# Attention's four key heads: a loop of one written pass and three repeated passes becomes four written passes on TensorE, ScalarE and VectorE

## The reference

```python
q = rope(x @ Wq + bq)   # 16 heads of 128, G = 4 query groups of HKV = 4 heads
k = rope(x @ Wk + bk)   # 4 key heads
v = x @ Wv + bv
scores = einsum('bgjtd,bjsd->bgjts', q, k) * scale      # j: the key head
wei = softmax(where(causal, scores, -inf))
out = einsum('bgjts,bjsd->bgjtd', wei, v)
x = layernorm(x + out @ Wo + bo)
x = layernorm(x + experts(x))     # top 8 of 64 experts per token
```

## Time and profile before

| what | us |
|---|---|
| median of 3 runs | 2161.45 |
| lowest and highest of them | 2160.99, 2162.3 |
| the profiled execution's own time | 2163.78 |
| span of the profiled execution, first to last instruction | 2162.0 |
| PE busy | 2042.1 (94%) |
| PEld busy | 1808.2 (84%) |
| DVE busy | 1679.5 (78%) |
| ACT busy | 1369.5 (63%) |
| POOL busy | 851.0 (39%) |
| mean granted TensorE clock | 0.978 |

### The profile page before, as it was taken

The page is one execution under the profiler, slowest core; times in us unless marked ns, Lnnn a source line. Parts: engine busy times, 40 slices in busy tenths (PEclk is TensorE's granted clock), DMA queues, the critical chain, the costliest instruction groups (busy, mean ns, idle before and its releaser), DMA issues. The chain is left out here.

```text
span 2162.0 us, 41335 instructions
## 1 busy us (share of the span) xinstructions
PE 2042.1 (94%) x13409; PEld 1808.2 (84%) x13409; DVE 1679.5 (78%) x3483; ACT 1369.5 (63%) x2747; POOL 851.0 (39%) x813
## 2 busy tenths in 40 slices
PE   8999989999999999999999999899959999999990
PEld 6888878998888988889888999788748999999990
DVE  5899987877678776787767877578877888888884
ACT  3677776766667666676656766332326877777773
POOL 1000013332233332333223333044455777787773
PEclk9999999999999999999999999999979999999995
DMA  7558553110531105301062000667637999999997
GB/s 241 189 209 287 217 210 111 61 64 21 158 115 41 59 21 174 111 30 59 22 225 99 29 21 21 241 242 287 235 112 218 298 299 297 296 292 293 296 250 257
DMA packets 140266, 362.62 MB, mean 168 GB/s; under 512 B 16304, under 2 KB 33328, under 8 KB 135472
## 3 DMA queue, kind: packets, MB, share of 16 engines
q1 hardware_dynamic: 111408, 292.09, 38.5%
q0 software_dynamic: 28672, 68.17, 13.2%
HBM read 224.27 MB, written 135.94 MB: 167 GB/s over the span
## 5 line engine op out<-in xcount | busy, mean ns | idle before, releaser
L654 PE MATMUL p_S<-p_kT,p_q 128*128 128x512 f32 (+3 forms) x1920 | 474.0, 377 | 14.0 <-ACT p_prob L732 12.0
L654 PEld LDWEIGHTS p_S<-p_kT,p_q 128*128 128x128 f32 x1920 | 324.2, 190 | 62.9 <-ACT p_prob L732 17.6
L843 POOL TENSOR_SCALAR p_prob<-p_prob,p_inv 128x128 f32<-128x128 f32 (+7 forms) x256 | 192.7, 753 | 452.3 <-DVE p_inv L792 452.3
L843 POOL TENSOR_SCALAR p_prob<-p_prob,p_inv,p_part 128x1024 f32<-128x1024 f32 x128 | 153.7, 1201 | 494.3 <-DVE p_inv L797 494.3
L666 PE MATMUL p_TP<-p_ident,p_prob 128*128 128x128 f32 x2176 | 303.6, 274 | 1.8 <-DVE p_pT1l L803 1.8
L781 DVE TENSOR_REDUCE p_nmax<-p_S 128x1 f32<-128x1024 f32 (+7 forms) x256 | 252.0, 984 | 22.8 <-PE p_S L654 21.8
L666 PEld LDWEIGHTS p_TP<-p_ident,p_prob 128*128 128x128 f32 x2176 | 245.5, 141 | 26.0 <-DVE p_pT1l L803 5.6
L741 ACT CAST p_pT0h<-p_TP 128x512 fp32r<-128x512 f32 (+3 forms) x320 | 155.3, 527 | 147.7 <-PE p_TP L666 146.6
L741 ACT CAST p_pT1h<-p_TP 128x512 fp32r<-128x512 f32 (+3 forms) x320 | 154.9, 526 | 145.7 <-PE p_TP L666 145.5
L1656 POOL DMA_INDIRECT sum_scratch<-p_y,p_tokT x128 | 212.9, 1663 | 55.7 <-issue 37.5
L689 PE MATMUL p_O<-p_pT1h,p_v 128*128 128x256 f32 x1088 | 225.9, 292 | 3.2 <-DVE p_pT0l L803 3.1
(11 more groups left out here) (228 smaller groups left out, 4555.8 us busy)
## 6 DMA issues: line engine op xcount, KB each, us to landing
p_w_raw<-in_gu SPq DMA_DIRECT2D x64, 768.0 KB
qk_scratch<-p_qout SPq DMA_DIRECT2D x80, 512.0 KB, 2.8
p_q<-qk_scratch SPq DMA_DIRECT2D x16, 2048.0 KB, 8.9
o_scratch<-p_oT SPq DMA_DIRECT2D x128, 256.0 KB, 2.1
p_ot<-o_scratch SPq DMA_DIRECT2D x32, 1024.0 KB, 7.4
p_w_raw<-in_gu SPq DMA_DIRECT2D x64, 256.0 KB
v_scratch<-p_vout SPq DMA_DIRECT2D x16, 512.0 KB, 3.2
p_t_raw<-in_dn SPq DMA_DIRECT2D x32, 256.0 KB
```

Of the source, the lines that this page charges most:

```text
L654: mm = nc.tensor.matmul(out, x, y, start=(n == 0), stop=(n == 2))
L843: nc.gpsimd.tensor_scalar(prob[k][:, cols], prob[k][:, cols], inv[:, k:k + 1], scale, ALU.mult, ALU.mult).then_inc(normed, 1)
```

## The change

`steps` no longer calls `loop`. The four heads are written out by Python for the three engines that call it, with j a number in all of them. GpSimd's loop and SyncE's loop stay as they are.

```diff
         def steps(eng, step, tail):
-            def body(j, first):
+            for j in range(HKV):
                 for i in range(U):
-                    step(j, i, first)
-            loop(eng, HKV, body)
+                    step(j, i, j == 0)
             for i in range(U, U + tail + 1):
                 step(HKV - 1, i, False)
```

## The result

Over 20 runs each the changed kernel has a median of 2158.07 us (2155.85 to 2162.29) and the kernel before 2161.82 us (2158.25 to 2163.98). The ratio is 0.9981, with a 95% interval of 0.9975 to 0.9988: the change gains 0.12 to 0.25%, or 2.6 to 5.4 us. That is clear over 20 runs each, but two single runs could not tell it, since the ranges overlap. The forecast was 2158.2 and a gain of 3.25 us; the medians differ by 3.75.

The account below looks back on a forecast made before the run. PE was taken as the bound, busy 2042.1 of 2162.0 us. From a median of 2161.45, -4.64 for branches and +1.39 for constants make -3.25, giving 2158.2 us; range 2154.8 to 2160.6.

Parts of the forecast that it names:

- The branches: Passages from head 1 to 2 and 2 to 3: without taken branches they lose 2.34 and 2.30 us, 4.64 in all.
- the second hole: Passage from head 1 to 2: PE idles 0.86 us for the key copy behind VectorE's branch; 0.98 us at the next.
- The constants: Heads 1 to 3: constants instead of registers in the waits cost 0.46 us per head, 1.39 us in all.
- Rival A: Heads 1 to 3: constants cost nothing, head 0's slower steps come from its place; 2156.8 us, chance 0.22.
- the hole at step 9: Head 3, step 9: PE waited 2.01 us, with a store late behind SyncE's 3 MB load; forecast to stay near 2.0.
- The fetch of the longer stream: Heads 1 to 3 as straight code: instruction fetching costed at nothing, covered by queued matmuls; otherwise up to 1.61 us per packet.
- Rival D: Heads 1 to 3: straight code starves PE, slower by over 0.2%; 2170.8 us at 0.3 us per packet, chance 0.05.
- ScalarE's branches: Passages between heads: removing them costed at nothing by itself, since ScalarE waits there for PE's transposes.
- SyncE's and GpSimd's: Loops kept on these engines: GpSimd's branch is hidden, SyncE's issues hang on semaphores that move with the heads; no cost.
- Rival C: Passages keep their length, set by GpSimd's or SyncE's branch or the like; nothing won, constants cost 1.39; 2162.8 us, chance 0.08.
- Rival B: Head 3, step 9: PE's 2.01 us hole closes too, up to 2.0 us more gained; 2156.2 us, chance 0.10.

Follow-up runs that it names:

- one branch left: Against the kernel before: heads 0 and 1 written out, heads 2 and 3 in a two-pass loop on TensorE, ScalarE and VectorE; 2158.05 us, ratio 0.9984.
- VectorE alone: Against the kernel before: only VectorE's heads written out, TensorE and ScalarE keep their loops; 2159.56 us, ratio 0.9985.
- TensorE alone: Against the kernel before: only TensorE's heads written out, ScalarE and VectorE keep their loops; 2166.10 us, ratio 1.0012.

## Why the prediction was right

**The branches (forecast -4.64 us).** The passages lost 0.16, 2.50 and 2.46 us, 5.12 in all. 4.64 of it are as forecast, and the experiments show both causes: one branch left leaves one long passage; VectorE alone removes the second hole; TensorE alone turns both into one. I had mis-sized one term by 0.48: the passage without a branch was taken as the floor, at 6.75, and the floor is 6.58. In the kernel before the scores of head 1 start at 545.78, 0.23 us after the key copy ends (544.87 + 0.68), in the changed kernel at 810.34, 0.05 after it (809.60 + 0.69). In between the sequencer of the register form has two instructions for its waits at that place, at 545.6 (L645, 37 ns) and 545.7 (L648, 32 ns). That it is TensorE's form is shown by the first passage of the experiments: 6.58 or 6.59 us wherever TensorE is written out, alone too, and 6.74 with VectorE alone. So here, where PE truly waits, the register form costs 0.16 to 0.18 us; the prediction had said that its instructions lie wholly beside matmuls.

**The constants (forecast +1.39 us).** Steps 13 to 63 grew by 0.39, 0.40 and 0.36 us in heads 1 to 3, and steps 0 to 13 by 0.08 and 0.07 in heads 1 and 2: together 1.30, or about 1.4 us with head 3's first steps taken alike. The size is right, and so is the mechanism: the swap of two waits takes it back and more. Rival A, that constants cost nothing, is out: heads 1 to 3 of the changed kernel are 228.1 us, as head 0 always was. But the name was only half right. It is not the constant form but which wait is written last. (The sum took 51 steps where 13 to 63 are 50; that is 0.03 us in the term.)

**The rest.** Steps 0 to 13 of head 3 became 0.17 us shorter, since the hole at step 9 came out smaller, and those of head 0 0.17; head 0's other steps and the tail changed by 0.03 and -0.02. The 0.34 us of the first steps lie within what these vary between profiles, so they are no gain of the change. Sum for attention: -5.12 + 1.15 + 0.15 - 0.34 + 0.01 = -4.15, against 4.16 measured. The medians of the runs differ by 3.75, between this and the forecast.

**How near the time came.** That 2158.2 met 2158.07 so closely is in part luck. The 2161.45 it started from, a median of three runs, is 0.37 us under the median of twenty, and the gain was put 0.50 us too low; the two errors nearly cancel. Nor does the time decide for the forecast: its interval of 2.6 to 5.4 us holds Rival A's gain of 4.64 too. What decides is the rows, which show each of the two terms.

**What was costed at nothing.** The fetch of the longer stream: the larger queue moved 14, 16 and 15 packets in heads 0, 1 and 2 of the changed kernel, and there is no new hole of PE, so Rival D is out. Over the whole execution the two instruction queues moved 95 and 65 packets, where the kernel before has 101 and 85 on its page: four written passes brought no more to fetch than the loop. ScalarE's branches: nothing, shown by keeping them. SyncE's and GpSimd's: nothing, shown by removing them, and with that Rival C is out too. Rival B's hole stayed, and its cause is now known.

**The weighed rules.** What the Trainium skill says in Runtime: NRT & Kernel Launch, Instruction fetch mechanics, that a taken branch out of the pages on chip stops the stream for a fetch, held in the three kernels in which PE still branches over a long body: five taken branches of 3304 to 3865 ns in PE's sequencer, against 67 to 83 ns where a compare and branch falls through. That it is the fetch that fills this time is the rule's word; no run here separates it. The 108 ns that the Trainium skill gives in Advanced Engine Details and Errata, Control Flow Timing, fit neither these nor the 208 ns of the short loops.

## What to carry to other kernels

Where a kernel has one written pass and a loop over the same work, the trace already holds both forms: compare equal steps, and the passage with a branch to the one without, before unrolling anything. A taken branch of a long loop body cost an engine 2.4 to 3.9 us of its stream here; it reached the end only where that engine had no work queued or another waited for what stands right behind the branch. So write out together the engines whose holes follow one another: VectorE alone gained 3.1 us by the medians of its chip, TensorE alone lost 3.5. ScalarE, GpSimd and SyncE had slack and gained nothing. Of two constant waits on a matmul, write last the one that is met long before.

## What the runs showed of the hardware that was not expected

TensorE alone was slower than the change's parts explain. Its windows around the passage from head 1 to 2, with the columns of the earlier trace rows, and the same passage's end in PE's timeline:

```profile
811.00:814.20 3.20, 0.83 (x8) 0.48 (x6) 0.79 (x2) 1.62 (x4) 0.00 (x0) 0.91 0.03 8
814.20:817.60 3.40, 3.40 (x16) 3.40 (x17) 1.81 (x5) 0.46 (x2) 1.52 (x2) 0.50 0.00 0
817.60:821.00 3.40, 3.40 (x20) 3.40 (x19) 1.45 (x3) 1.45 (x3) 0.77 (x1) 0.58 0.00 0
```

```profile
814.88 0.33 PE L660 MATMUL p_S<-p_maskb,p_identb 128*128 128x128 bf16 x1
```

From the end of the one wait of 2.37 us the granted clock was at 0.50, that is 1.2 GHz, until about 820.5 (0.58 over the last window), and the mask product took 0.33 us where it takes 0.23 at 2.4 GHz. Step 1 of head 2 took 7.58 us there instead of 5.26, and in head 3, after a wait of 2.24 us, 6.60 (granted clock 0.57 from 1086.5 to 1090.5). That is 3.7 us for two waits that are together no longer than the holes of the kernel before. There, the same idle time came in two pieces with work between them, and the granted clock of heads 1 and 2 was 1.00. So a wait that is only moved and joined to another can cost more than before.

It needs no branch. In VectorE alone the old hole at step 9 of head 3 came out at 2.30 us, and the clock fell behind it; PE's timeline and the window:

```profile
1105.09 1.01 PE L658 MATMUL p_S<-p_kT,p_q 128*128 128x384 f32 x3 [2.30 <-ACT p_prob L736]
```

```profile
1105.00:1109.00 4.00, 3.91 (x18) 3.28 (x19) 2.61 (x9) 2.43 (x9) 1.26 (x3) 0.57 0.48 155
```

Steps 0 to 13 of head 3 took 34.11 us there against 32.84 in the kernel before, 0.29 of it by the longer hole, so some 1 us by the clock. Behind the holes of 2.01 us and 1.77 us of the kernel before and the changed kernel, at the same place, the granted clock stayed at 1.00. That the waits bring the clock down is read from the order of the rows in these three cases; no experiment was made for it.
